# Two expert loops of a four-layer Perceiver block written out as streams of half steps, with the next stage's inputs loaded during the first

## Time and profile before

| | us |
|---|---|
| median of 3 runs | 4496.87 (4488.52 to 4499.94) |
| profiled execution | 4495.25 |
| its span | 4493.5 |
| TensorE busy | 3684.8 (82% of the span) |
| VectorE busy | 2284.9 (51%) |
| ScalarE busy | 1752.8 (39%) |
| GpSimd busy | 697.2 (16%) |

### The profile page before, as it was taken

One profiled execution on the slowest core, in us unless ns is written; L12 is line 12 of the kernel. 1 busy time (PEld: TensorE's weight loads), 2 busy tenths in 40 slices (PEclk: granted clock), 3 DMA queues, 4 the chain that ended last, 5 costly groups with the idle time before them and its releaser, 6 DMA issues. The chain is left out here.

```text
span 4493.5 us, 91372 instructions
## 1 busy us (share of the span) xinstructions
PE 3684.8 (82%) x38096; PEld 2594.8 (58%) x38096; DVE 2284.9 (51%) x4483; ACT 1752.8 (39%) x3460; POOL 697.2 (16%) x351
## 2 busy tenths in 40 slices
PE   6999998788878499997568886999996989986654
PEld 4666666556655277785334454777775755543333
DVE  5666666655442277765834354555555232231157
ACT  4666665222211277774513341444441211111124
POOL 2676764100000000000201011011110000000011
PEclk9999999899989799999878898999997689998877
DMA  2010100111100424430010001111110001127600
GB/s 68 31 46 31 46 31 17 46 33 33 33 3 28 163 98 147 143 132 13 0 41 0 0 0 41 49 49 49 49 33 20 1 29 35 34 79 245 236 22 13
DMA packets 173595, 243.62 MB, mean 54 GB/s; under 512 B 40001, under 2 KB 152447, under 8 KB 173128
## 3 DMA queue, kind: packets, MB, share of 16 engines
q1 hardware_dynamic: 173256, 238.65, 16.1%
HBM read 237.58 MB, written 1.05 MB: 53 GB/s over the span
## 5 line engine op out<-in xcount | busy, mean ns | idle before, releaser
L2554 POOL TENSOR_TENSOR x_sc<-x_sc,h_T 128x2048 f32<-128x2048 f32 (+1 forms) x105 | 442.5, 4248 | 252.9 <-ACT h_T L2762 252.9
L2374 ACT ACTIVATE x_sc<-x_sc,x_nb 128x2048 f32<-128x2048 f32 (+1 forms) x112 | 210.6, 1880 | 297.7 <-DVE x_sc L2423 297.5
L2837 DVE TENSOR_TENSOR x_most<-x_most,ps 128x512 f32<-128x512 f32 (+1 forms) x352 | 234.8, 685 | 80.2 <-PE ps L2670 68.0
L2423 DVE SCALAR_TENSOR_TENSOR x_sc<-ps,x_nb,x_cap 128x2048 f32<-128x2048 f32 (+1 forms) x112 | 246.2, 2198 | 49.5 <-PE ps L2315 49.5
L1417 ACT ACTIVATE s_both<-ps,s_less,s_rs_s 128x64 f32<-128x64 f32 x624 | 214.0, 425 | 70.1 <-DVE s_less L1523 70.1
L2741 ACT COPY x_sc<-ps 128x1024 f32<-128x1024 f32 x192 | 179.3, 945 | 133.4 <-PE ps L2670 86.1
L2627 PE MATMUL ps<-x_wv,x_ctx_T 128*128 128x256 f32 (+1 forms) x832 | 206.9, 391 | 0.0
L2755 ACT ACTIVATE x_sc<-x_sc 128x2048 f32<-128x2048 f32 (+1 forms) x112 | 201.2, 1797 | 4.1 <-DVE x_sc L2554 4.0
L2286 PE MATMUL ps<-x_ctx_T,x_wk 128*128 128x401 f32 (+1 forms) x512 | 200.0, 517 | 1.5 <-PEq L44 1.5
L2619 PE MATMUL ps<-x_ctx_T,x_wk 128*128 128x401 f32 (+1 forms) x512 | 196.9, 523 | 3.4 <-POOL x_v L2583 3.4
L2294 PE MATMUL ps<-x_wv,x_ctx_T 128*128 128x256 f32 (+1 forms) x832 | 197.7, 379 | 0.0
(11 more groups left out here) (516 smaller groups left out, 7705.1 us busy)
## 6 DMA issues: line engine op xcount, KB each, us to landing
x_ctx_T<-in_ctx_T SPq DMA_DIRECT2D x50, 1601.0 KB
x_ctx_n<-in_ctx SPq DMA_DIRECT2D x18, 1536.0 KB
s_ctx_T<-in_ctx_T SPq DMA_DIRECT2D x16, 1601.0 KB, 10.4
s_ctx_n<-in_ctx SPq DMA_DIRECT2D x16, 1536.0 KB
h<-in_ctx SPq DMA_DIRECT2D x12, 896.0 KB, 5.1
e_w<-in_L_attn_W SPq DMA_DIRECT2D x8, 1024.0 KB
rows<-in_ctx SPq DMA_DIRECT2D x12, 640.0 KB
f_wg<-in_L_w_gate SPq DMA_DIRECT2D x18, 256.0 KB
```

The costliest lines, as they stand in the source:

```text
L2374: nc.scalar.activation(x, x, ACT.Square, scale=DH ** -0.5, bias=nb[0:keys, 0:1]).then_inc(squared, 1)
L2423: nc.vector.scalar_tensor_tensor(out=slot[0:keys].rearrange("p r m h j q -> p (r m h) (j q)")[:, :, 0:width], in0=score_banks[0:keys].rear ...
L2554: return eng.tensor_tensor(x, x, most_of, ALU.subtract)
L2837: ins = nc.vector.tensor_tensor(best[0:keys, rs], best[0:keys, rs], score_banks[0:keys, rs, :, j, :], ALU.max)
```

## The change

- `expert` and its two loops go. A class `Experts` writes down an order of half steps: up of one half of the tokens, then down of the half before the last, and so on over all experts (`up(a,0) up(a,1) down(a,0) up(b,0) down(a,1) up(b,1) down(b,0)` ...). `run_experts` writes this out as one block for each feed-forward, with constant addresses.
- PSUM: up groups use four banks as a ring (four groups deep with one matrix, two with gate and up); down steps use the other four, two tiles to a bank, two steps in turn. VectorE waits for both tiles of a bank before it adds the first.
- Weights have two buffers each. SyncE loads the expert after next when the up products, or the down products, of the one two back are done. The first expert's weights are no longer loaded during the layernorm, but at the start of the stream.
- Routing moves into the stream: the gate matmuls after the first up step, the counting matmuls after the first down step of layer 0, VectorE's chain beside them. The turning of the weights and the second bias become steps of their own behind expert 4. In layer 2 the shared expert comes first.
- The block `s1_in` goes. Its buffers are allocated before the first feed-forward (`L1Inputs`); GpSimd clears four pads, SyncE issues the ten weight loads after the first two experts' weights, and then one of eight parts of the context for each expert. One pad is cleared by GpSimd in the next stage.

```diff
+class Experts:
+    def __init__(self, order, n_in, extra_ups=(), extra_downs=()):
+        self.ring = 4 // n_in
+        ups = [("up", e, c) for e in self.order for c in range(2)]
+        downs = [("down", e, c) for e in self.order for c in range(2)]
+        seq = ups[0:1]
+        for u, w in zip(ups[1:], downs):
+            seq += [u, w]
+        seq += downs[-1:]
...
+def run_experts(...):
+            @block.sync
+            def _(sp):
+                for i, e in enumerate(order):
+                    if i >= 2:
+                        old = ("up", order[i - 2], 1)
+                        sp.wait_ge(product, n_in * (plan.group(old, KT - 1) + 1))
+                    for dst, src in loads_in(e, i % 2):
+                        sp.dma_start(dst, src).then_inc(in_sem[i % 2], 16)
+                    if i >= 2:
+                        sp.wait_ge(down, plan.down_count(("down", order[i - 2], 1), 3))
+                    for dst, src in loads_out(e, i % 2):
+                        sp.dma_start(dst, src).then_inc(out_sem[i % 2], 16)
+                    more_loads(sp, i, own)
+            @block.tensor
+            def _(pe):
+                for item in plan.seq:
+                    if kind == "up":
+                        if c == 0:
+                            pe.wait_ge(in_sem[i % 2], 16 * n_loads_in * (i // 2 + 1))
+                        for m in range(KT):
+                            if g >= plan.ring:
+                                pe.wait_ge(hidden, g - plan.ring + 1)
...
+                    elif kind == "down":
+                        if c == 0:
+                            pe.wait_ge(out_sem[i % 2], 16 * n_loads_out * (i // 2 + 1))
+                        pe.wait_ge(hidden, plan.group(("up", e, c), KT - 1) + 1)
+                        for j, t in enumerate(plan.tiles(item)):
+                            if plan.down_at[item] >= 2 and j % 2 == 0:
+                                pe.wait_ge(added, plan.down_count(item, j) - 7)
...
+                    pe_part(pe, item, own, product, hidden, down, added)
+            @block.scalar
...
+                            if number[e] > 0:
+                                act.wait_ge(down, plan.down_count(
+                                    ("down", order[number[e] - 1], c), 3))
+                            act.wait_ge(product, n_in * g + 1)
+            @block.vector
...
+                            if j % 2 == 0:
+                                dve.wait_ge(down, plan.down_count(item, j + 1))
+                            if plan.added_before(item, j):
+                                dve.wait_ge(added, plan.added_before(item, j))
 def l0_ffn(nc, env, d):
+    env.l1 = next_inputs = L1Inputs(nc, env, d)
-            (b2[:, :], d["L0_ffn_b2"]),
-            (w1[:, :, :], wview(d["L0_ffn_W1"][0]))])
+            (b2[:, :], d["L0_ffn_b2"])])
+        TURN, BIAS = ("turn", None, 0), [("bias", None, c) for c in range(2)]
+        plan = Experts(range(E), 1, extra_ups=[(("up", 4, 0), TURN)],
+                       extra_downs=[(("down", 4, c), BIAS[c]) for c in range(2)])
+        def more_loads(sp, i, own):
+            if i == 1:
+                sp.wait_ge(next_inputs.cleared, 4)
+                next_inputs.load_weights(sp)
+            if i >= 1:
+                next_inputs.load_part(sp, i - 1)
+            if i == E - 1:
+                next_inputs.load_part(sp, i)
+        def pe_part(pe, item, own, product, hidden, down, added):
+            if item == ("up", 0, 0):    # gate matmuls, bank 7
...
+            elif item == ("down", 0, 0):
+                pe.wait_ge(picked, 1)   # counting matmuls, bank 6
...
+            elif item == ("up", 1, 0):
+                pe.wait_ge(weighed, 1)
...
-        with nc.Fori(0, E) as e:
-            expert(nc, env, "f0_expert", [w1], ...)
 def l1_xattn(nc, env, d):
-        with signals(nc, "s1_in", ...):    # the loading block
...
+    given = env.l1
 def l2_ffn(nc, env, d):
+        plan = Experts([E, *range(E)], 2)
+            if item == FIRST:               # gate matmuls after up(E, 0), bank 7
...
-        with nc.Fori(0, E + 1) as e:
-            expert(nc, env, "f2_expert", [wg, wu], ...)
+        run_experts(nc, env, "f2_experts", plan, w_in, wd, None, hid_T, weigh, ...)
```

More of the change, by code:

```diff
@@ L357, in _, with group, up_bank, down_bank @@
                                             ALU.add).then_inc(added, 1)
[L360 to L367, removed]
+class Experts:
+    def __init__(self, order, n_in, extra_ups=(), extra_downs=()):
+        self.n_in, self.order = n_in, list(order)
+        self.ring = 4 // n_in
[5 more added lines that the diff above has]
+        seq += downs[-1:]
+        for after, item in extra_ups + extra_downs:
+            seq.insert(seq.index(after) + 1, item)
+        self.seq = seq
+        self.up_at = {x: i for i, x in enumerate(x for x in seq if x[0] in ("up", "turn"))}
+        self.down_at = {x: i for i, x in enumerate(x for x in seq if x[0] in ("down", "bias"))}
+    def group(self, item, m):
+        return KT * self.up_at[item] + m
+    def up_bank(self, item, m):
+        return self.n_in * (self.group(item, m) % self.ring)
+    def down_bank(self, item, i):
+        return 4 + 2 * (self.down_at[item] % 2) + i // 2
+    def tiles(self, item):
+        return [4 * item[2] + i for i in range(4)]
+    def down_count(self, item, i):
+        return 4 * self.down_at[item] + i + 1
+    def added_before(self, item, i):
+        old = [x for x in self.down_at if x[2] == item[2]
+               and self.down_at[x] < self.down_at[item]]
+        return self.down_count(old[-1], i) if old else 0
@@ new lines, in run_experts @@
+def run_experts(nc, env, stage, plan, w_in, w_out, bias, hid_T, weigh, loads_in, loads_out,
+                more_loads, names, pool_part, pe_part, act_part, dve_part):
+    n_in, order = plan.n_in, plan.order
+    n_loads_in, n_loads_out = len(loads_in(0, 0)), len(loads_out(0, 0))
+    with signals(nc, stage, "in_even in_odd out_even out_odd product silu hidden down added "
+                 + names) as sems:
+        in_even, in_odd, out_even, out_odd, product, silu, hidden, down, added = sems[0:9]
+        own = sems[9:]
+        in_sem, out_sem = (in_even, in_odd), (out_even, out_odd)
+        number = {e: i for i, e in enumerate(order)}
@@ L384, in _ @@
+            @block.gpsimd
+            def _(pool):
+                pool_part(pool, own)
             @block.tensor
             def _(pe):
[L386 to L393, removed]
@@ L929, in l0_ffn @@
         hid_T, comb_T = sb("hid_T", [P, KT, N]), sb("comb_T", [E, N])
+        ps = env.ps
         layernorm(nc, env, "f0_ln", env.x, env.h, env.h_T, loads=[
             (gate[:, :, :], wview(d["L0_ffn_gate_w"])), (b1[:, :, :], d["L0_ffn_b1"]),
[L932 to L1008 removed]
@@ new lines, in act_part @@
+        def act_part(act, item, own, product, hidden):
+            logits, steps_in, shifted, exped, picked, counted, weighed = own
+            if item == ("up", 0, 0):
+                act.wait_ge(shifted, 1)
+                nc.scalar.activation(probs[:, :, :], probs[:, :, :], ACT.Exp).then_inc(exped, 1)
+            elif item == TURN:
+                for c in range(2):
+                    act.wait_ge(product, plan.group(TURN, c) + 1)
+                    nc.scalar.copy(comb_T[:, c * NH:(c + 1) * NH],
+                                   ps[0:E, plan.up_bank(TURN, c), :]).then_inc(hidden, 1)
@@ new lines, in no_part, with pe_part @@
+        def no_part(*_):
+            pass
+        def pe_part(pe, item, own, product, hidden, down, added):
+            steps_in, logits, exped, routed = own
+            if item == FIRST:
+                for t in range(T):
+                    for k in range(KT):
+                        last = nc.tensor.matmul(ps[:, 7, t * E:(t + 1) * E],
+                                                env.h_T[:, k, t * P:(t + 1) * P],
+                                                gate[:, k, :], start=(k == 0),
+                                                stop=(k == KT - 1))
+                last.then_inc(logits, 1)
+            elif item == ("up", 0, 0):
+                pe.wait_ge(exped, 1)
```

462 lines of the change are left out of this document (265 added, 197 removed).

## The result

The changed kernel takes 4388.07 us (median, 4383.46 to 4397.17) against 4498.4 for the kernel before: a ratio of 0.976, 95% interval 0.974 to 0.978. Its profiled execution took 4384.93 us (span 4383.2) against 4495.25, so 110.3 us less. Forecast were 4395 us, and 101.6 less.

What follows compares the result with a forecast made beforehand. It took TensorE's work plus a barrier each turn, and 37.0 us of pure loading, as the bound. Stretches summing to 129.0 and 363.5 us save 62.9 and 38.7, together 101.6, giving 4395 us; range 4386 to 4422.

Steps and rivals of the forecast that it cites:

- the two stretches: Start of routing to next layernorm, first and third feed-forward: 191.9 to 129.0 us and 402.2 to 363.5.
- wait for the first weights: At each stream's start TensorE waits for loads formerly hidden under the layernorm: 2.6 us first, 3.5 third.
- experts' products: Up and down matmuls without stops between half steps: 8 times 13.77 us is 110.1; 17 times 20.63 is 350.7.
- slow clock at the start: First matmuls of each stream run slower: 2 us taken in each, bounds 1.6 to 6.
- gate matmuls: Routing matmuls inside each stream, taken midway between full and half clock: 5.2 us, bounds 3.5 to 7.0.
- counting matmuls: Sixteen routing matmuls in the first stream, taken midway between clock levels: 2.6 us, bounds 1.7 to 3.6.
- transposes and bias: First stream, at full clock: transposes 1.0 us and bias matmuls 3.4.
- tail and boundary: End of each stream: last pair of additions 1.2 us, then 0.9 to the layernorm.
- The loading block leaves the path: Next-stage loads behind the first feed-forward, 37 us, move under TensorE's stream and cost nothing there.
- neighbour waits: Rival: TensorE waits about 1.0 us for neighbouring half steps at 150 places in both streams; 4545 us, chance 0.03.
- VectorE's additions: Additions of down products in the streams now go in pairs, 0.97 us a pair.
- Code arrives late: Rival: new code of 25 expert bodies stalls TensorE 1.2 us each; 4425 us, or about 4410; chance 0.09.

Runs made afterwards that it cites:

- late_inputs: Changed kernel with all next-stage inputs issued in a block of their own after the first stream; 4423.3 us (one run).
- early_weights: Changed kernel with the first expert's up weights loaded beside the layernorm again, in both streams; 4382.78 us, ratio 0.976.
- unrolled_blocks: Kernel before with its two expert loops written out, blocks and barriers kept, addresses constant; 4472.94 us (one run).
- gate_first: Changed kernel with the gate matmuls ahead of the first up products, in the wait for the first weights; 4389.94 us (one run).
- pile: Changed kernel with all eight parts of the next stage's inputs issued at once behind the ten weight loads; 4407.69 us (one run).
- ring_one: Changed kernel in which each up group waits for the group before, a ring of one; 4448.6 us (one run).

## Why the prediction was right

The forecast of 4395 us was 7 us high. The measured 4388 lies inside the stated range, 4386 to 4422, but near its lower end, and 1 us below the 4389 to 4415 that the bounds of the terms alone gave. 3.2 us of the 7 are in the two stretches; the rest lies in the untouched stages, 5.5 us shorter in the profile, and between runs. Those stages scatter over 11 us, from 3868.7 to 3879.8, so the mechanism was right, but that the whole came so close is in part luck. Term by term, forecast and then measured:

| term | first, forecast | first, measured | third, forecast | third, measured |
|---|---|---|---|---|
| wait for the first weights | 2.6 | 2.9 (4.39 - 1.50) | 3.5 | 3.7 (5.19 - 1.50) |
| experts' products | 110.1 | 110.2 (8 x 13.78) | 350.7 | 350.9 (17 x 20.64) |
| slow clock at the start | 2 | 2.3 (1337.88 to 1343.64, less 3.44) | 2 | 1.5 (3544.52 to 3552.90, less 6.88) |
| gate matmuls | 5.2 | 3.5 | 5.2 | 3.5 |
| counting matmuls | 2.6 | 1.7 | | |
| transposes and bias | 4.4 | 4.7 | | |
| tail and boundary | 2.1 | 1.7 | 2.1 | 1.7 |
| stretch, from the start of routing | 129.0 | 127.8 | 363.5 | 361.5 |

The measured terms of the first stretch sum to 127.0; the remaining 0.8 us lie in the small restarts where the kind of matmul changes. The steps that carry the sum held. Products at the pace of one turn without its barrier: within 0.1%. The loading block leaves the path and nothing takes its place (`late_inputs`, where it costs 35.4 us again). The cost that the change adds, the wait for the first weights, is there and of the size read from SyncE's waits in the old loop (`early_weights` takes it away). What was off is one size: I took the middle between the two clock levels for the narrow matmuls, and they ran at the higher one (granted clock 1.00 in 1343.6 to 1347.1), 4.3 us less over both streams.

Two things I had priced without need or wrongly. The rival on the other side, neighbour waits, was put at 4545 us, with a wait at 150 places. Made true for the up groups it bites at 50, because a down step covers each other group, and the kernel is then still 45 us faster than before. It could not have decided the sign in this form; the waits of the down steps I did not try. And VectorE's additions go at 0.88 us a pair in the stream, not 0.97.

"Code arrives late" was a rival of 0.09. No gap without a cause lies in the streams, and the DMA view of the first one shows 4 packets on the two instruction queues beside 13,815 of the loads. In the changed kernel the unexplained stops are in the unrolled stage behind them, as before:

```profile
PE ps L1444 <- issue: 3.3, 2, 2.9
PE ps L1455 <- issue: 1.4, 1, 1.4
```

The rule of the Trainium skill ("Runtime: NRT & Kernel Launch", section "Instruction fetch mechanics"), that code streams ahead and its fetch is mostly hidden, fits these streams and `unrolled_blocks`, where written-out turns became 0.55 us shorter. The same section warns that a taken branch whose target lies outside the two blocks at hand stalls for a fetch. The sign of these 0.55 us agrees, but a turn has only 48 matmuls and 48 weight loads on TensorE (384 of each in 8 turns), so whether the condition was met is not shown. Run-time addresses went at the same time, and which of the two it was is open.

Where the 104.8 us come from: 35.4 the loading block, 5.3 + 10.8 the loops as such, and the remaining 53.3 the block ends of 25 turns and the routing that now lies behind and beside matmuls at the higher clock. No run takes these last two apart. An estimate from the turns: 25 times 1.50 us (15.28 less 13.78, 22.14 less 20.64) is about 37 for the block ends, which leaves some 16 for the routing, less what the wait for the first weights costs.

## What to carry to other kernels

Price a loop whose turns end in a barrier by one turn's matmuls, from the start of the first to the end of the last less the overlap that the trace shows, times the turns; what the turn takes beyond that is what a stream gives back, as long as nothing else in it has to wait. Here the loads of the next stage were free beside dense matmuls because they were dealt out, one portion per expert and behind the weights that are due sooner; in one pile they held the issuing queue. When a stage's first weights move into the stream, look for the wait at its head: loading them beside the layernorm as before took 3.3 and 3.5 us away here.

## What the runs showed of the hardware

- The 32 matmul records of the gate (float32, 8 columns, each with its own weight load) took 6.97 us at the lower clock level (granted clock 0.50, `gate_first`) and 3.63 behind dense ones at the higher (1.00, the changed kernel). One of these weight loads took 333 ns in the one and 192 in the other.
- The issue of a 65 KB load held SyncE for 3.85 us in the changed kernel and up to 11.11 us in `pile`, each time with 1.5 MB loads issued ahead of it.
- A turn of a loop with branch and run-time addresses took 0.55 us more than the same turn written out: 15.83 against 15.28, and 22.69 against 22.14.
- In `ring_one` a wait that held TensorE for 0.83 to 0.85 us cost 1.2 us of its stream on average.
- 123 us of dense float32 matmuls kept their pace with the DMA engines moving 157 GB/s beside them (123.15 us) and without these loads (123.22).
